# A CIN tower on one core: x0 for G comes back through DRAM instead of PE transposes, the dense rows are padded to 128, G's columns are in group order, and there are four block slots

## The reference

```
e = stack([tbl_f[ids[:, f]] for f in range(39)])           # [1024, 39, 16]
Xi = e
for W, b in (W0, b0), (W1, b1), (W2, b2):
    Xi = einsum('hjk,bjd,bkd->bhd', W, e, Xi) + b          # [1024, 128, 16]
    res.append(Xi.sum(axis=2))
h = concat(res + [dense_ctx])                              # [1024, 400]
h = relu(h @ W_top1 + b_top1); h = relu(h @ W_top2 + b_top2); y = h @ W_top3
```

## Time and profile before

| | us |
|---|---|
| median of 3 runs (lowest, highest) | 1438.17 (1437.16, 1438.38) |
| the profiled execution | 1436.21 |
| its span in the trace | 1434.40 |
| mean granted TensorE clock | 0.972 of full |

### The profile page before, as it was taken

The page is one execution under the profiler, slowest core; times in us unless marked ns, Lnnn a source line. Parts: engine busy times, 40 slices in busy tenths (PEclk is TensorE's granted clock), DMA queues, the critical chain, the costliest instruction groups (busy, mean ns, idle before and its releaser), DMA issues.

```text
span 1434.4 us, 23609 instructions
## 1 busy us (share of the span) xinstructions
PE 1313.6 (92%) x6157; PEld 1061.7 (74%) x6157; DVE 1082.4 (75%) x2678; ACT 1066.5 (74%) x3372; POOL 892.8 (62%) x663
## 2 busy tenths in 40 slices
PE   3179999999999999999999999999999999999986
PEld 3158777777788777887778777887778878887765
DVE  3068989898867987688766988679876988679930
ACT  2238888789867887688867888678876899678942
POOL 6658577868766678666766587667776265341111
PEclk8659999999999999999999999999999999999999
DMA  6242222322221222303231122212232122210010
GB/s 214 51 111 57 51 64 71 84 55 53 72 80 33 65 59 64 76 21 77 62 88 46 44 62 60 80 33 71 53 90 55 29 67 71 78 31 8 9 38 0
DMA packets 53451, 87.27 MB, mean 61 GB/s; under 512 B 15136, under 2 KB 37152, under 8 KB 52032
## 3 DMA queue, kind: packets, MB, share of 16 engines
q1 hardware_dynamic: 43172, 82.64, 21.4%
q0 software_dynamic: 9984, 2.58, 1.9%
q10 hardware_dynamic: 156, 0.48, 0.1%
HBM read 18.47 MB, written 8.39 MB: 19 GB/s over the span
## 4 chain that ended last, share of the span: by engine, by line
PE 54%; POOL 19%; issue 12%; DVE 8%; DMA 3%; ACT 2%; SPq 1%; ACTq 0%; POOLq 0%; DVEq 0%
PE ring L927 12%; PE ring L929 11%; PE ring L928 11%; POOL pairs L396 6%; POOL pairs_lo L407 6%; PE side L825 5%; POOL e_in L364 5%; PE l_ps L812 3%; DVE terms L754 3%; POOL blocks L418 3%; PE side L851 3%; PE l_ps L814 3%; PE l_ps L813 2%; DVE x_s L709 2%; DMA x_rep<-x_t 2%
## 5 line engine op out<-in xcount | busy, mean ns | idle before, releaser
L597 ACT ACTIVATE terms<-ring,e_both 128x128 f32<-128x128 f32 x2944 | 832.2, 399 | 242.9 <-PE ring L929 237.4
L754 DVE SCALAR_TENSOR_TENSOR terms<-ring,e_both,terms 128x128 f32<-128x128 f32 x1792 | 508.4, 344 | 96.7 <-PE ring L929 93.6
L927 PE MATMUL ring<-w_hi,x_hi 128*128 128x512 f32 (+1 forms) x1280 | 546.4, 427 | 32.5 <-DVE terms L754 25.2
L929 PE MATMUL ring<-w_hi,x_lo 128*128 128x512 f32 (+1 forms) x1280 | 500.4, 391 | 0.0
L928 PE MATMUL ring<-w_lo,x_hi 128*128 128x512 f32 (+1 forms) x1280 | 498.8, 390 | 0.0
L709 DVE TENSOR_REDUCE x_s<-terms 128x32 f32<-128x800 f32 x512 | 489.0, 976 | 0.2
L364 POOL DMA_INDIRECT e_in<-in_tbl,idx x312 | 305.8, 980 | 88.6 <-issue 79.0
L407 POOL TENSOR_TENSOR pairs_lo<-pairs,pairs_hi 117x1024 fp32r<-117x1024 f32 (+1 forms) x104 | 250.0, 2404 | 168.0 <-ACT pairs_hi L497 167.0
L927 PEld LDWEIGHTS ring<-w_hi,x_hi 128*128 128x128 f32 x1280 | 242.9, 190 | 106.8 <-DVE terms L754 38.5
L396 POOL TENSOR_TENSOR pairs<-x_rep,pairs 117x1024 f32<-117x1024 f32 (+1 forms) x104 | 250.4, 2408 | 93.2 <-DMA pairs<-x_t 93.2
L928 PEld LDWEIGHTS ring<-w_lo,x_hi 128*128 128x128 f32 x1280 | 243.6, 190 | 49.1
(11 more groups left out here) (64 smaller groups left out, 629.1 us busy)
## 6 DMA issues: line engine op xcount, KB each, us to landing
pairs<-x_t SPq DMA_DIRECT2D x312, 156.0 KB
x_scratch<-x_s SPq DMA_DIRECT2D x32, 256.0 KB, 2.2
x_r<-x_scratch SPq DMA_DIRECT2D x8, 1024.0 KB, 6.0
x_rep<-x_t SPq DMA_DIRECT2D x45, 156.0 KB
g_t<-in_L_rec_W SPq DMA_DIRECT2D x2, 2496.0 KB, 10.3
e_in<-in_tbl,idx POOLq DMA_INDIRECT x312
x_r<-x_t SPq DMA_DIRECT2D x8, 156.0 KB
wtop<-in_W_top SPq DMA_DIRECT2D x1, 768.0 KB
```

Of the source, the lines that this page charges most:

```text
L597: last = nc.scalar.activation(term(d, ACT_BEFORE[d][g] + i), twos(ring[:, (GROUPS * d + g) % RING, i * H:(i + 1) * H]), ACT.Copy, scale=e_ ...
L754: nc.vector.scalar_tensor_tensor(out=acc, in0=y, scalar=e_of[:, j, d:d + 1], in1=acc, op0=ALU.mult, op1=ALU.add).then_inc(dve_unit, 1)
L927: nc.tensor.matmul(acc, x1_hi[:, x], w1_hi[:, w], start=True, stop=False)
L929: nc.tensor.matmul(acc, x1_lo[:, x], w1_hi[:, w], start=False, stop=True).then_inc(y_group, 1)
```

## The change

- `xb` no longer comes from PE. SP writes `e_cur` to a DRAM scratch after loading pair tile 11 (`x0_write`) and reads it back in the layout of `xb` at the start of the next step (`xb_back`). The transposes, the two ACT copies and the waits on them go. `e_cur` is laid out [d, f] instead of [f, d], so that a row of the scratch (39 words) is contiguous. One `xb` buffer is left.
- Blocks are laid out [field, sample] instead of [sample, field], in four slots. A result of G then has its 8 samples side by side, and ACT writes them to 8 neighbouring columns: `g_t`, z0, z2, h1 and the dense features keep the samples in the order of the groups; h2 is put back in order when ACT copies it.
- The dense features and their rows of W_top1 are padded with zeros to 128 rows (two DVE memsets at the start), so the fourth matmul of H1 has 128 rows. The DMA of those 16 rows comes after the memsets in SP's queue.
- SP's steps are unrolled; the other engines keep the loop.

```diff
-    XB_SLICES, XB_AT = (0, 1), 6
-    BLOCK_FIRST, BLOCK_SLOTS = 7, 3
+    BLOCK_FIRST, BLOCK_SLOTS = 7, 4
-    X2_LAST_AFTER = 9
+    X2_LAST_AFTER, X0_AFTER = 9, 11
-        e_cur = e_both[:, WRAPPED:WRAPPED + FIELDS, :]
+        e_cur = e_both[:, WRAPPED:WRAPPED + FIELDS, :].rearrange("p f d -> p (f d)").rearrange(
+            "p (d f) -> p d f", f=FIELDS)
-        xb = [sb(f"xb{i}", [P, G_GROUPS, FIELDS]) for i in range(2)]
-        blocks = sb("blocks", [P, BLOCK_SLOTS, SAMPLES_PER_G, GCOLS])
+        xb = sb("xb", [P, G_GROUPS, FIELDS])
+        blocks = sb("blocks", [P, BLOCK_SLOTS, GCOLS, SAMPLES_PER_G])
+        x0_dram = nc.dram_tensor("x0_scratch", [D, P, FIELDS], f32, kind="Internal").ap()
+        def by_group(ap):
+            return ap.rearrange("p (g b) -> p b g", b=SAMPLES_PER_G)
SP:
-            sp.dma_start(wtop1[0:DENSE, 3, :], W_top1[3 * P:, :]).then_inc(top_in, 16)
...
+            sp.wait_ge(dense_cleared, 2)
+            sp.dma_start(wtop1[0:DENSE, 3, :], W_top1[3 * P:, :]).then_inc(top_in, 16)
+                def x0_write():
+                    after(sp, e_cur_ready, c + 1)
+                    after(sp, xb_in, 16 * c)
+                    sp.dma_start(x0_dram.rearrange("d b f -> b d f"), e_cur).then_inc(x0_out, 16)
+                def xb_back():
+                    after(sp, x0_out, 16 * c)
+                    after(sp, block_made, G_GROUPS * (c - 1))
+                    sp.dma_start(xb[:, :, :], x0_dram.rearrange("d (b g) f -> (d b) g f", g=G_GROUPS)
+                                 ).then_inc(xb_in, 16)
+                if previous:
+                    xb_back()
                 if mlp:
...
                             x2_back()
+                        if i == X0_AFTER:
+                            x0_write()
-            steps(sp, step)
+            steps(sp, step, unrolled=True)
POOL, make_block:
-                        after(pool, xb_ready, 2 * c)
+                        after(pool, xb_in, 16 * c)
-                    shape = [P, SAMPLES_PER_G, FIELDS]
+                    shape = [P, FIELDS, SAMPLES_PER_G]
                     nc.gpsimd.tensor_tensor(
-                        blocks[:, g % BLOCK_SLOTS, :, 0:FIELDS],
-                        xb[1 - odd][:, g:g + 1, :].to_broadcast(shape),
-                        own[:, :].unsqueeze(2).to_broadcast(shape), ALU.mult).then_inc(block_made, 1)
+                        blocks[:, g % BLOCK_SLOTS, 0:FIELDS, :],
+                        xb[:, g, :].unsqueeze(2).to_broadcast(shape),
+                        own[:, :].unsqueeze(1).to_broadcast(shape), ALU.mult).then_inc(block_made, 1)
ACT:
-                        nc.scalar.activation(e_cur[:, :, :], e_mid[:, 0:FIELDS, :], ACT.Copy).then_inc(e_cur_ready, 1)
+                        after(act, x0_out, 16 * c)
+                        nc.scalar.activation(e_cur, e_mid[:, 0:FIELDS, :].rearrange("p f d -> p d f"),
+                                             ACT.Copy).then_inc(e_cur_ready, 1)
-                        g_t[:, :, g::G_GROUPS],
-                        side[:, g % 2, 0:SAMPLES_PER_G * GCOLS].rearrange("p (b j) -> p j b", j=GCOLS),
+                        g_t[:, :, g * SAMPLES_PER_G:(g + 1) * SAMPLES_PER_G],
+                        side[:, g % 2, 0:SAMPLES_PER_G * GCOLS].rearrange("p (j b) -> p j b", j=GCOLS),
-                    if layer1 and e in XB_SLICES:
...
-                        nc.scalar.activation(xb[odd][:, n * q:n * (q + 1), :], side[:, 1, 0:n * FIELDS],
-                                             ACT.Copy).then_inc(xb_ready, 1)
-                        nc.scalar.activation(dense_t, side[0:DENSE, 1, 0:P], ACT.Copy).then_inc(dense_ready, 1)
+                        nc.scalar.activation(by_group(dense_t[0:DENSE, :]),
+                                             side[0:DENSE, 1, 0:P].rearrange("p (b g) -> p b g", g=G_GROUPS),
+                                             ACT.Copy).then_inc(dense_ready, 1)
DVE:
+            nc.vector.memset(dense_t[:, :], 0.0).then_inc(dense_cleared, 1)
+            nc.vector.memset(wtop1[:, 3, :], 0.0).then_inc(dense_cleared, 1)
-                    nc.vector.tensor_reduce(dst, l0_ps[:, :].rearrange("p (d b) -> p b d", b=P),
-                                            AX.X, ALU.add).then_inc(z0_summed, 1)
+                    nc.vector.tensor_reduce(
+                        by_group(dst), l0_ps[:, :].rearrange("p (d b g) -> p b g d", b=SAMPLES_PER_G, g=G_GROUPS),
+                        AX.X, ALU.add).then_inc(z0_summed, 1)
PE:
-                    if layer1 and d in XB_SLICES and g == XB_AT:
...
-                            last = nc.tensor.transpose(side[:, 1, i * FIELDS:(i + 1) * FIELDS],
-                                                       x0_t[0:FIELDS, r::G_GROUPS],
-                                                       ident[0:FIELDS, 0:FIELDS])
-                            rows = DENSE if k == 3 else P
                             last = nc.tensor.matmul(side[:, 1, m * P:(m + 1) * P],
-                                                    wtop1[0:rows, k, m * P:(m + 1) * P], z,
+                                                    wtop1[:, k, m * P:(m + 1) * P], z,
                                                     start=(k == 0), stop=(k == 3))
```

More of the change, by code:

```diff
@@ L230, in build_tower, with scale_of @@
         block = ctx.enter_context(nc.Block())
+        def by_group(ap):
+            return ap.rearrange("p (g b) -> p b g", b=SAMPLES_PER_G)
+        def scale_of(j, d):
+            return e_mid[:, j, d:d + 1] if d < CUR_FROM else e_cur[:, d, j:j + 1]
         def twos(ap):
@@ L243, in after, with steps @@
                 eng.wait_ge(semaphore, count)
-        def steps(eng, step):
+        def steps(eng, step, unrolled=False):
             step(-1, 1, layer1=False, following=True, previous=False, mlp=False, gathers=True)
@@ L248, in steps @@
             step(1, 1, layer1=True, following=True, previous=True, mlp=False, gathers=True)
-            with eng.Fori(2, CHUNKS - 3, 2) as c:
-                step(c, 0, layer1=True, following=True, previous=True, mlp=True, gathers=True)
-                step(c + 1, 1, layer1=True, following=True, previous=True, mlp=True, gathers=True)
+            if unrolled:
+                for c in range(2, CHUNKS - 2):
+                    step(c, c % 2, layer1=True, following=True, previous=True, mlp=True, gathers=True)
+            else:
+                with eng.Fori(2, CHUNKS - 3, 2) as c:
+                    step(c, 0, layer1=True, following=True, previous=True, mlp=True, gathers=True)
+                    step(c + 1, 1, layer1=True, following=True, previous=True, mlp=True, gathers=True)
             step(CHUNKS - 2, 0, layer1=True, following=True, previous=True, mlp=True, gathers=False)
@@ L549, in side_work @@
                         for m in range(M2 // P):
-                            last = nc.scalar.activation(h2_sb[:, m, :], side[:, 0, m * P:(m + 1) * P], ACT.Relu,
-                                                        bias=btop2[:, m:m + 1])
+                            last = nc.scalar.activation(
+                                h2_sb[:, m, :].rearrange("p (b g) -> p b g", g=G_GROUPS),
+                                by_group(side[:, 0, m * P:(m + 1) * P]), ACT.Relu, bias=btop2[:, m:m + 1])
                         last.then_inc(h2_ready, 1)
@@ L632, in _ @@
                                     ALU.add).then_inc(own_made, 1)
+            nc.vector.memset(dense_t[:, :], 0.0).then_inc(dense_cleared, 1)
+            nc.vector.memset(wtop1[:, 3, :], 0.0).then_inc(dense_cleared, 1)
             dve.wait_ge(own_made, 1)
             for i in range(BLOCK_SLOTS):
-                last = nc.vector.tensor_copy(blocks[:, i, :, FIELDS], own[:, :])
+                last = nc.vector.tensor_copy(blocks[:, i, FIELDS, :], own[:, :])
             last.then_inc(own_made, 2)
@@ L725, in step @@
                     n = D * c + d
-                    e_of = e_mid if d < CUR_FROM else e_cur
                     if layer1 and d == 0:
@@ L828, in side_work @@
                                 last.then_inc(z2_ps, 1)
-                    if layer1 and d in XB_SLICES and g == XB_AT:
-                        q = XB_SLICES.index(d)
-                        n = G_GROUPS // 2
-                        for i in range(n):
-                            r = q * n + i
-                            last = nc.tensor.transpose(side[:, 1, i * FIELDS:(i + 1) * FIELDS],
-                                                       x0_t[0:FIELDS, r::G_GROUPS],
-                                                       ident[0:FIELDS, 0:FIELDS])
-                        last.then_inc(xb_ps, 1)
                     if mlp and d == DENSE_SLICE and g == GROUPS - 1:
                         after(pe, dense_in, 16 * (c - 1))
-                        if layer1:
-                            after(pe, xb_ready, 2 * (c + 1))
+                        after(pe, g_ready, G_GROUPS * (c - 1))
```

(5 more changed lines are left out.)

26 lines of the change are left out of this document (10 added, 16 removed).

## The result

The changed kernel took 1390.05 us (median of four, 1388.79 to 1391.06), the one before 1438.28 (1437.16 to 1438.90): a ratio of 0.9665, 95% interval 0.9648 to 0.9682. 1390 was forecast. The profiled executions differ by 1434.40 - 1386.9 = 47.5 us of span; 48.0 was forecast.

A forecast was written before the change was run, and what follows sets the result against it. PE, busy 92% of the span, was taken as the bound. 18.9 + 11.5 + 15.0 + 2.6 = 48.0 us off the 1438.2 us median gives 1390.2 us, range 1382 to 1406.

The forecast's parts named there:

- Transposes: Slices 0 and 1 of all 8 steps: PE loses 16 bursts of eight transposes at 1.18 us, 18.9 us gone.
- Dense rows: H1 groups on PE: 128 rows instead of 16 bring H2's price, 0.36 us less a group, 11.5 us in all.
- row count does not matter: Rival for H1's dense passes: padding to 128 rows brings nothing, time 1402 us; chance 0.08.
- Fourth slot: Slices 10 to 15 of steps 1 to 5: POOL's blocks stop waiting for G, 3.0 us a step, 15.0 us.
- it isn't late next: Slice 10 of step 2: ACT's high part ends at 508.54, so it would not be the next thing late.
- the bound of 1.1 us: POOL's blocks: the forecast is wrong if they pass 1.1 us; the rival that POOL is still late had chance 0.10.
- Steps 8 and 9: After the gathers end: 2.3 us from four blocks made ahead plus 0.3 us from ACT's copy of G, together 2.6 us.
- I take halfway, 0.3 us: ACT's copy of G in steps 8 and 9: reads in order, writes in runs of eight, saving 0.3 us (0 to 0.6).
- What is added: The e_cur copy, DRAM write and read back, dense-row DMA, memsets, reordered copies and SP unrolling: nothing, at worst 0.5 us a step.
- Anything under 20 us is hidden: The DRAM write ahead of pair tile 12 in the queue: a write under 20 us costs nothing; about 5 us expected.
- The rival's price: Rival: the DRAM write holds the queue, stopping slice 4 in 8 steps; at 32 us it costs 96 us, 1486; chance 0.04.
- L812 on POOL down to about 7 waits: Sign in the changed profile: PE's waits for the pair tiles' low parts from POOL fall from 27 to about 7.

The follow-up runs named there:

- e3: The changed kernel with three block slots and 16-row H1 dense passes, leaving x0 through DRAM and the new column order: 1466.16 us, ratio 0.9829 to the kernel before.
- e4: The kernel before with only H1's dense passes padded to 128 rows: 1480.82 us, ratio 0.9918 to the kernel before.
- e2: The changed kernel with H1's dense passes at 16 rows again: 1453.19 us, ratio 0.9744 to the kernel before.
- e2b: The changed kernel with H1's dense passes at 64 rows instead of 128: 1402.2 us, ratio 0.9754 to the kernel before.
- e1: The changed kernel with three block slots instead of four: 1456.58 us, ratio 0.9746 to the kernel before.
- e11: The changed kernel, four slots kept, with ACT's copy of G reading its bank with a step again: 1392.27 us, ratio 0.9689 to the kernel before.
- e8: The changed kernel with the DRAM write of e_cur issued six times, five to tensors nobody reads: 1492.63 us, ratio 1.0381 to the kernel before.

## Why the prediction was right, and where it was not

- *Transposes, 18.9 us:* right, in slices 0 and 1 of every step. e3 keeps it without the rest.
- *Dense rows, 11.5 us:* right in size and cause. e4 gives it in the old kernel, e2 and e2b take it back. The rival "row count does not matter", with the rule of the Trainium skill ("TensorE: Matmul & The Clock Gate", "Why this matters for your kernels") beside it, falls: a pass of 64 or 16 rows between passes of 128 costs 0.37 us a group. The rule speaks of one matmul by itself. What costs is going from 128 rows to 64 or 16 and back. The skill's "TensorEngine Tiling (Array Packing)", "Key Properties", says that a change of tiling mode drains TensorE: the trace agrees, with a gap on both sides at 64 rows and none at 117.
- *Fourth slot, 15.0 us:* 14.6, and e1 gives it back. Its worth, read from step 6, was good to 0.2 us a step. The reason given for step 6 was wrong: it has the wait on POOL too, six times, 1.9 to 3.2 us each (one is shown below). What it lacks is gathers, so that the low part is in time all the same and PE doesn't wait. ACT's high part does come next, against the prediction's "it isn't late next": POOL waits 0.73 us for it in slice 10 of step 2, and PE's slices 10 to 14 take their 9.26 us all the same. POOL's wait in step 6 of the kernel before:

```profile
1161.60 0.72 POOL L418 TENSOR_TENSOR blocks<-xb,own 128x312 f32<-128x312 f32 x1 [1.91 <-PE side L898]
```

- *Blocks:* the bound of 1.1 us was not needed, they take 0.73 us with runs of 8.
- *Steps 8 and 9, 2.6 us:* the sum was right and its split wrong. "With four made ahead and 0.70 us each without waits, the last of 12 ends at 1402.5: 2.3 us" failed: e1 shows nothing for the slot. "I take halfway, 0.3 us" failed too: the copy takes 454 ns (median; writing in runs of eight costs nothing), and it paced the whole stretch, 2.2 us, with 0.4 us more ahead of step 8's z2. The copy of the dense features, put at "nothing within 0.1 us", makes PE begin H1 0.13 us later in each of steps 8 and 9. The short waits of 0.28 us between pairs of blocks came from ACT's copy two places back: they are gone with the fast copy at three slots (e1) and there with the slow one at four (e11).
- *What is added, nothing:* right. The `e_cur` copy takes 1.33 us (up to 1.3 forecast) and shows nowhere. The write lands after 7.2 us (5 forecast).
- *"Anything under 20 us is hidden":* right for steps 2 to 7, by e8 20.4 to 21.4 us; in steps 0 and 1 it is 13 and 17. The rival's price, 8 x 12 = 96 us for a write that takes 32 us, compares with e8's 105 us for writes of 31.7 to 33.8 us, the excess being in steps 0 and 1. By e8's figures the turning point lies at 25 us, forecast 26. One write lands after 7.2 us, so this rival stayed unlikely.
- *L812 on POOL down to about 7 waits:* 11. Slice 9 of steps 1 to 5 stayed at 10.1 to 10.2 us, as forecast. The two unforeseen terms, +2.5 and -2.4 us, cancelled: that the total met the forecast to 0.2 us is chance, that it met it within 3 us is not.

## What to carry to other kernels

Look for a step of the same kernel in which the busiest engine lacks the wait in question: the difference in length is the price of the wait, better than any sum over queues. Check in the rows what that step really lacks. Where two engines alternate with short waits, follow each wait one more place back before giving a buffer the credit; a faster evacuation may be the whole gain. And when you load a queue, read the landings and not the issues: SP had issued all six writes after 22 us, and they had landed after 32.

## What the runs showed that was not expected

- A pair of H1 passes with 64 rows costs as much as one with 16: 0.37 us more in a group, at entering and leaving. Passes of 117 rows beside 128 cost nothing extra.
- ACT copies 320 words a partition out of a bank in 0.46 us in order and 0.77 with a step; out of SBUF, 624 words take 0.74 in order and 1.33 when read with a step. In the first pair the slow copy's writes step too. Writing in runs of eight words costs nothing.
- Next to bursts of gathers ACT and DVE stall on one chip and not on another: with 11 gathers in slices 6 and 7, slice 7 of steps 2 to 5 takes 11.7 to 12.0 us on one and 7.7 on the other; with 15 it takes 18.6 to 20.4 on the first, and was not run on the other. The changed kernel's times differ by 57 us between the chips, 25 of them in the set-up.
- A write of 2048 pieces of 156 bytes to DRAM lands after 7.2 us; six in a row need 32 us, some 4.6 us for each further one.
- Unrolling removed 2.3 to 2.8 us at the turn of the loop, and on the chip with the stalls 17.5 us more.
